# The first head's mask, in half of the key tiles, multiplied in by GpSimd after the exponential; both mask tables written by VectorE

## The chip, the core and the metric

The kernel runs on one core of a Trainium2 chip. The core has five engines with a queue each: TensorE (PE in the profile; its weight loads are PEld), VectorE (DVE), ScalarE (ACT), GpSimd (POOL) and SyncE (SP), which here only issues DMAs. They meet through semaphores. The metric is the device time of one execution in microseconds; smaller is better.

## The reference, cut to what matters

Four layers follow each other on `x` (4 batches, 512 queries, 256 features): a cross attention, an expert layer, a second cross attention with a mask over 1601 keys and 16 heads of 16 features, and a routed expert layer. The change touches the second cross attention alone:

```
energy = einsum('nqhd,nkhd->nhqk', qp, kp)                    # 4 batches, 16 heads, 512 x 1601
energy = where(mask == 0, -1e20, energy)
attention = softmax(energy / sqrt(256), axis=3)
out = einsum('nhql,nlhd->nqhd', attention, vp) @ fo_w.T + fo_b
```

The mask is one table of 512 x 1601 integers for each batch, the same for all its heads.

## The kernel before, in words

The second cross attention is the function `attention_c`. Its work is cut into 16 groups (`G` from 0 to 15; batch `b = G // 4`, and `g = G % 4` counts the four groups of four heads of a batch) and each group into 13 tiles of 128 keys (`i` from 0 to 12, the last with 65 keys). `T = 13 G + i` numbers the 208 tiles. For each tile and each of the four heads `h`, TensorE writes the scores, keys on the partitions and 512 queries along the free side, into one bank of PSUM (`score`, L2021); ScalarE takes the exponential with the scale in it into `prob` (L2189); and TensorE multiplies four heads' `prob` with the values, which carry a column of ones for the row sums (`values`, L2042). `prob` has two slots, one for each parity of `T`.

The exponential needs the row maximum. TensorE computes the scores of the *next* group a second time, queries on the partitions (`maximum`, L1995: 32 units `u` per group, two matmuls each), and VectorE adds the mask and takes the maximum of each unit (L2216, a main instruction and a read of its accumulator). Two units are under way at most: unit `m` waits on TensorE until VectorE is done with unit `m - 2`. At a group's end the maxima are split into three bf16 parts, turned and copied to the query rows, so that the score matmul subtracts them.

The mask comes into the scores in one of three ways, written down by `bank_plan` (L1613) for each tile and head in `MASKS`:

- `pe`: a matmul of an identity with the tile of `maskT` (0 or -1e20, bf16) opens the bank, and the score matmul adds to it (L2038, then L2039);
- `act`: ScalarE copies the tile of `maskT` into the bank ahead of the score matmul (L2185);
- `dve`: VectorE does so (L2306), in the last group only.

Over the 832 pairs of tile and head that is 498 `pe`, 310 `act` and 24 `dve`. Heads 0 and 1 are nearly always `pe`, heads 2 and 3 mostly `act`.

The order on TensorE within a tile is: scores of heads 0 and 1, a maximum unit, the values of the tile before, score of head 2, a maximum unit, score of head 3, a maximum unit. With three units per tile the 32 units are done after tile 10, and tiles 11 and 12 have none. Single jobs of the rest of the layer (turning outputs, projections, queries of the next batch, routing) lie between tiles of groups with `g` 0 and 1.

`maskT` is made from the integer mask, which is loaded two tiles at a time into one of two slots of `c_rawT`. GpSimd writes it (`bias_t`, L1908): all 13 tiles of batch 0 at the layer's start, and those of the next batch in group `g = 3` (tiles 2 to 10) and at the start of the following `g = 0`. GpSimd also scatters rows into `table` by indirect DMA for the routed layer (128 of them, L260), fills `table` with zeros in group 2 (16 DMAs, L1965, two each in tiles 2 to 9), copies values (L1874) and splits queries. Its loop over the tiles waits for the first score matmul of each tile, then runs `beside` (L1920).

## Time and profile before

| | before |
|---|---|
| median of 3 runs | 2099.51 us (2098.49 to 2099.77) |
| span of the profiled execution | 2122.9 us |
| the layer's tiles (first score matmul to last values) | 1100.9 to 1883.5 us of the span |
| busy in the span: PE / DVE / ACT / POOL | 1982.3 / 1269.1 / 893.8 / 528.3 us |
| VectorE maxima L2216 | 480 units, 467.7 us and 66.8 us of accumulator reads |
| ScalarE exponentials L2189 and mask copies L2185 | 832 and 310 |
| TensorE mask matmuls L2038 | 498 |
| GpSimd mask tiles L1913 | 52, 100.2 us |

The profile gives no other time for the profiled execution than its span; it is 23.4 us over the median of the runs. Matmuls are pipelined, so their durations overlap: what one costs TensorE is read as the distance from its start to the next start, not from its duration. The same holds, to a smaller degree, for ScalarE and VectorE.

### The profile page before, as it was taken

The numbers are of one execution on the slowest core, as the hardware profiler recorded it, in microseconds if no ns is written. First come the engines' busy times: TensorE is split into PE (matmuls) and PEld (weight loads), VectorE is DVE, ScalarE is ACT, GpSimd is POOL, SyncE is SP. The second block draws the span as 40 slices with busy tenths as digits, with TensorE's granted clock in tenths as the row PEclk, the third lists the DMA queues.
The fourth block names the chain that finished last, engine by engine and source line by source line (L and its number), as shares of the span: only waits on it lengthen the run. The fifth ranks groups of instructions, "written<-read, shape, count | busy, mean of one in ns | idle before, by whom it ended". The sixth has DMA issues, their size and how long they took to land. (4 is left out here: it accounts for less than half of the span.)

```text
span 2122.9 us, 27241 instructions
## 1 busy us (share of the span) xinstructions
PE 1982.3 (93%) x10186; PEld 1100.5 (52%) x10186; DVE 1269.1 (60%) x2541; ACT 893.8 (42%) x1791; POOL 528.3 (25%) x454
## 2 busy tenths in 40 slices
PE   7989999999999999899989999999999999965994
PEld 5666567745676567746643333433433343334773
DVE  5423765366633764367777777777776777741343
ACT  3412211221112211121118888778777977841221
POOL 4311000210001000000034223236324531426664
PEclk9999999999999999999999999999999999986997
DMA  8743000110001000110226383345335432215986
GB/s 286 213 200 111 1 1 11 45 43 1 1 21 62 1 1 11 34 28 16 44 79 129 85 259 81 80 120 123 90 70 146 104 57 43 73 62 164 251 182 157
DMA packets 101531, 184.97 MB, mean 87 GB/s; under 512 B 38151, under 2 KB 62549, under 8 KB 100120
## 3 DMA queue, kind: packets, MB, share of 16 engines
q1 hardware_dynamic: 83000, 153.24, 26.8%
q0 software_dynamic: 18400, 30.00, 6.3%
q8 instruction: 81, 1.33, 0.3%
q14 instruction: 50, 0.41, 0.1%
HBM read 127.38 MB, written 65.25 MB: 91 GB/s over the span
## 5 line engine op out<-in xcount | busy, mean ns | idle before, releaser
L2216 DVE CUSTOM_DVE_ANT_0 ps<-ps,maskN 128x801 f32<-128x801 f32 x480 | 467.7, 1014 | 129.5 <-PE ps L2009 126.3
L2189 ACT ACTIVATE d_prob<-ps 128x512 f32<-128x512 f32 (+1 forms) x832 | 473.4, 597 | 158.3 <-PE ps L2039 153.2
L856 PE MATMUL ps<-vx_or_keys,b_xT 128*128 128x512 f32 x512 | 240.3, 597 | 4.9 <-DVE val_or_prob L1209 4.9
L840 PE MATMUL ps<-oxB,og_or_pT 128*128 128x256 f32 x1024 | 241.1, 380 | 0.0
L2051 PE MATMUL ps<-d_prob,vaug 128*32 128x512 f32 (+1 forms) x1664 | 226.6, 610 | 0.3 <-ACT d_prob L2189 0.3
L840 PEld LDWEIGHTS ps<-oxB,og_or_pT 128*128 128x128 f32 x1024 | 190.5, 190 | 37.4 <-issue 11.2
L2038 PE MATMUL ps<-maskT,identb 128*128 128x512 bf16 (+1 forms) x498 | 192.2, 386 | 5.7 <-DVE d_oN L2248 1.7
L1095 ACT ACTIVATE prob_or_gate<-ps,b_mx 128x512 f32<-128x512 f32 (+3 forms) x128 | 66.1, 525 | 289.4 <-DVE b_mx L1200 289.4
L2185 ACT CAST ps<-maskT 128x512 f32<-128x512 bf16 (+1 forms) x310 | 185.6, 599 | 0.0
L260 POOL DMA_INDIRECT table<-xr,slot x128 | 128.6, 1005 | 177.5 <-PE ps L2039 140.8
L1209 DVE TENSOR_TENSOR val_or_prob<-ps,b_gm 128x512 f32<-128x512 f32 x128 | 88.4, 691 | 107.1 <-PE ps L856 107.0
L856 PEld LDWEIGHTS ps<-vx_or_keys,b_xT 128*128 128x128 f32 x512 | 93.5, 190 | 85.5 <-issue 77.5
L1213 DVE TENSOR_REDUCE val_or_prob<-val_or_prob 128x64 f32<-128x512 f32 x128 | 132.3, 1034 | 4.4
L2039 PE MATMUL ps<-raw,kS 99*128 99x512 bf16 (+1 forms) x312 | 115.7, 387 | 1.7 <-ACT ps L2185 1.7
L2038 PEld LDWEIGHTS ps<-maskT,identb 128*128 128x128 bf16 (+1 forms) x498 | 49.7, 100 | 123.0 <-issue 36.6
L1913 POOL TENSOR_SCALAR maskT<-c_rawT 128x512 bf16<-128x512 int32 (+1 forms) x52 | 100.2, 1926 | 49.0 <-PE ps L2039 42.2
L2039 PE MATMUL ps<-vx_or_keys 99*128 99x512 bf16 (+1 forms) x260 | 99.2, 385 | 1.9 <-ACT ps L2185 1.9
L2039 PE MATMUL ps<-qS,vx_or_keys 99*128 99x512 bf16 (+1 forms) x260 | 98.9, 384 | 1.9 <-ACT ps L2185 1.9
L670 PE MATMUL ps<-og_or_pT,raw 128*128 128x128 f32 (+1 forms) x832 | 97.6, 275 | 0.0
L640 PE MATMUL ps<-maskN,kS 128*128 128x512 f32 (+1 forms) x256 | 95.0, 519 | 1.7 <-PEq L98 1.7
L670 PEld LDWEIGHTS ps<-og_or_pT,raw 128*128 128x128 f32 (+1 forms) x832 | 95.4, 192 | 1.5 <-issue 1.5
L1332 DVE TENSOR_TENSOR og_or_pT<-b_oT,ps 128x512 f32<-128x512 f32 x128 | 81.9, 681 | 18.2 <-PE ps L814 18.2
(321 smaller groups left out, 2807.8 us busy)
## 6 DMA issues: line engine op xcount, KB each, us to landing
c_rawT<-in_maskT SPq DMA_DIRECT2D x24, 512.0 KB
vx_or_keys<-k_parts SPq DMA_DIRECT2D x60, 200.1 KB, 7.2
k_parts<-x_k SPq DMA_DIRECT2D x16, 600.4 KB
table<-xr POOLq DMA_DIRECT2D x16, 578.0 KB
e_buf<-table SPq DMA_DIRECT2D x32, 289.0 KB
raw<-in_mask SPq DMA_DIRECT2D x10, 800.5 KB, 4.2
vx_or_keys<-in_D_w SPq DMA_DIRECT2D x12, 640.0 KB, 5.5
e_w<-in_D_w SPq DMA_DIRECT2D x12, 640.0 KB
```

Of the source, the lines that this page charges most:

```text
L260: g.indirect_dma_start(out=k.table[:, :], out_offset=bass.IndirectOffsetOnAxis(ap=k.slot[:, j:j + 1], axis=0), in_=k.xr[:, t, :], in_offse ...
L670: mm = pe.matmul(ps[:, 6, m * P:(m + 1) * P], k.ctxNA[0:KW[i], i, m * P:(m + 1) * P], pT[0:KW[i], i, :], start=i == 0 and m == 0, stop=i = ...
L840: mm = pe.matmul(ps[:, 6 + t // 2, (t % 2) * D:(t % 2 + 1) * D], og[:, e, t * P:(t + 1) * P], oxB[:, p, e, :], start=first and t % 2 == 0, ...
L856: mm = pe.matmul(ps[:, bank, :], xTB[:, c, t * P:(t + 1) * P], vxB[:, c, h, :], start=c == 0, stop=c == NC - 1)
L1213: v.tensor_reduce(val[:, t, h // 2 % 2, h % 2, :], tmp[:, u % 2, :].rearrange("p (e d) -> p d e", e=EB), AX_X, ALU.add).then_inc(val_sum, 1)
L1913: g.tensor_scalar(maskT[0:KW[i], i, :], rawT[0:KW[i], u % 2, i % 2, :], 0.0, MASKED, ALU.is_equal, ALU.mult).then_inc(biasT, 1)
L2038: pe.matmul(ps[0:w, BANKS[u], :], k.identb[0:w, 0:w], maskT[0:w, i, :], start=True, stop=False)
L2039: pe.matmul(ps[0:w, BANKS[u], :], kS[G % NS][0:KROWS + 3, h, i * P:i * P + w], qS[G % NS][0:KROWS + 3, h, :], start=False, stop=True, skip ...
L2051: mm = pe.matmul(ps[VW * h:VW * (h + 1), ACC, :], vaug[0:w, G % 2, i, h, :], prob[0:w, T % 2, h, :], start=i == 0, stop=i == NKT - 1)
L2185: nc.scalar.copy(ps[0:w, BANKS[later], :], maskT[0:w, i, :]).then_inc(mask_a, 1)
L2189: nc.scalar.activation(prob[0:w, T % 2, h, :], ps[0:w, BANKS[GH * T + h], :], ACT.Exp, scale=SCALE_C).then_inc(exped, 1)
L2216: v.tensor_tensor_reduce(banks, banks, maskN[:, t, MO[half]:MO[half] + w], 1.0, -3.0e38, ALU.add, ALU.max, mp[:, t, h, half:half + 1]).the ...
```

## The change

A fourth way of masking, `cap`, is used for head 0 in 108 of the 208 tiles (`capped_by_gpsimd`). There TensorE writes the score of head 0 without a mask matmul, ScalarE takes the exponential of the unmasked score, and GpSimd then goes over the 128 x 512 tile of `prob` twice, in place: it bounds it by 2 and multiplies it by the tile of a second table `capsT` (1 for a seen key, 2^-100 for a hidden one). `values` waits for that (`capped`). In tiles with `i` divisible by 4 that are capped, head 2's mask goes from ScalarE's copy to TensorE's matmul. Both tables are written by VectorE, two instructions per tile, between its maxima: in group 0 two tiles ahead and then one behind each of the first 11 units; in groups with `g = 3` of batches 0 to 2 one behind every third unit from 6 to 30; and one behind units 2, 5, 8 and 11 of the following group. GpSimd's scatters are moved to tiles that are not capped. The tile into which `x` is loaded is now the one that holds the last `x` (`k.xl`). Over the pairs the plan now has 410 `pe`, 290 `act`, 24 `dve` and 108 `cap`.

```diff
@@ -1610,6 +1611,20 @@
+def capped_by_gpsimd(T):
+    G, i = divmod(T, NKT)
+    b, g = divmod(G, NG)
+    if g == 0:
+        return i != 12 and (b < 2 or i % 2 == 0 or i > 5)
+    if g == 1:
+        return 5 <= i <= 10
+    if g == 2:
+        return i >= 2 and (b == 0 or b + 1 < NB and i in (4, 6, 8, 10))
+    return b == 0 or b + 1 < NB and i in (2, 4, 6, 8, 10)
@@ -1650,11 +1665,15 @@
-                by = "pe"
-                if bank in whole:
+                by, cap = "pe", capped_by_gpsimd(NKT * G + i)
+                if h == 0 and cap:
+                    by = "cap"
...
-                    elif i >= 1 and G < NGB - 1 and h >= 2:
+                    elif i >= 1 and G < NGB - 1 and h >= (3 if cap and i % 4 == 0 else 2):
                         by = "act"
@@ -1905,13 +1931,18 @@
+            def cap(T):
+                by, count = MASKS[GH * T]
+                if by == "cap":
+                    w, i = KW[T % NKT], T % NKT
+                    p = prob[0:w, T % 2, 0, :]
+                    g.wait_ge(exped, GH * T + 1)
+                    g.tensor_scalar(p, p, 2.0, None, ALU.min).then_inc(bounded, 1)
+                    g.wait_ge(bounded, count)
+                    g.wait_ge(capT, NKT * (T // NKT // NG) + i + 1)
+                    g.tensor_tensor(p, p, capsT[0:w, i, :], ALU.mult).then_inc(capped, 1)
@@ -1933,17 +1964,19 @@
+                    if a == 2 and i >= 2 and b + 1 < NB:
+                        many = [1, 2, 0, 2, 0, 2, 0, 2, 0, 2, 1]
+                        scatters(b, sum(many[:i - 2]), many[i - 2])
+                    if a == 3 and b + 1 < NB:
+                        many = [1, 2, 0, 2, 0, 2, 0, 2, 0, 2, 0, 2, 1]
...
@@ -1974,21 +2005,17 @@
             for T in range(NKT * NGB):
                 g.wait_ge(s_mm, GH * T + 1)
                 beside(T // NKT // NG, T // NKT % NG, T % NKT)
+                cap(T)
@@ -2037,12 +2066,14 @@
                 pe.matmul(ps[0:w, BANKS[u], :], kS[G % NS][0:KROWS + 3, h, i * P:i * P + w], qS[G % NS][0:KROWS + 3, h, :],
-                          start=False, stop=True, skip_group_check=by != "pe").then_inc(s_mm, 1)
+                          start=by == "cap", stop=True, skip_group_check=by in ("act", "dve")).then_inc(s_mm, 1)
             def values(T):
                 pe.wait_ge(exped, GH * (T + 1))
+                if MASKS[GH * T][0] == "cap":
+                    pe.wait_ge(capped, MASKS[GH * T][1])
@@ -2269,13 +2300,34 @@
+            def bias_t(b, i):
+                u, w = NP * b + i // 2, KW[i]
+                v.wait_ge(ld_maskT[u % 2], 16 * (u // 2 + 1))
+                if b >= 1:
+                    v.wait_ge(s_mm, GH * (NKT * (NG * b - 1) + i + 1))
+                raw = rawT[0:w, u % 2, i % 2, :]
+                v.tensor_scalar(maskT[0:w, i, :], raw, 0.0, MASKED, ALU.is_equal, ALU.mult).then_inc(biasT, 1)
+                if b >= 1:
+                    v.wait_ge(capped, caps_until(NKT * (NG * b - 1) + i))
+                v.tensor_scalar(capsT[0:w, i, :], raw, 0.0, HIDDEN, ALU.not_equal, ALU.max).then_inc(capT, 1)
...
+                    if G == 0 and u < NKT - 2:
+                        bias_t(0, u + 2)
+                    if g == 3 and b + 1 < NB and 6 <= u <= 30 and u % 3 == 0:
+                        bias_t(b + 1, u // 3 - 2)
+                    if g == 0 and b >= 1 and u <= 11 and u % 3 == 2:
+                        bias_t(b, 9 + u // 3)
```

On TensorE, in tile 1 of group 0, this stood in a row before (L2038 mask, L2039 score, L2009 maximum, L2051 values):

```order
L2038 MATMUL ps<-maskT,identb 128x512
L2039 MATMUL ps<-raw,kS 128x512
L2038 MATMUL ps<-maskT,identb 128x512
L2039 MATMUL ps<-raw,kS 128x512
L2009 MATMUL ps<-vx_or_keys 128x512
L2009 MATMUL ps<-vx_or_keys 128x288
L2051 MATMUL ps<-d_prob,vaug 32x512 x4
```

and this stands there now (L2067 mask, L2068 score, L2082 values):

```order
L2068 MATMUL ps<-raw,kS 128x512
L2067 MATMUL ps<-maskT,identb 128x512
L2068 MATMUL ps<-raw,kS 128x512
L2040 MATMUL ps<-vx_or_keys 128x512
L2040 MATMUL ps<-vx_or_keys 128x288
L2082 MATMUL ps<-d_prob,vaug 32x512 x4
```

One mask matmul of the two ahead of the maximum is gone. On VectorE, at the start of group 0, the maxima (two rows each, `ISA`) followed each other directly before:

```order
L2237 COPY raw<-ps 3x1024 x2
L2216 ISA ps,d_mp<-ps,maskN 128x801
L2216 ISA d_mp 128x1
L2216 ISA ps,d_mp<-ps,maskN 128x800
L2216 ISA d_mp 128x1
```

and now have two pairs of table writes ahead of them and one pair behind each:

```order
L2268 COPY raw<-ps 3x1024 x2
L2311 TENSOR_SCALAR maskT<-c_rawT 128x512
L2314 TENSOR_SCALAR capsT<-c_rawT 128x512
L2311 TENSOR_SCALAR maskT<-c_rawT 128x512
L2314 TENSOR_SCALAR capsT<-c_rawT 128x512
L2247 ISA ps,d_mp<-ps,maskN 128x801
L2247 ISA d_mp 128x1
L2311 TENSOR_SCALAR maskT<-c_rawT 128x512
L2314 TENSOR_SCALAR capsT<-c_rawT 128x512
L2247 ISA ps,d_mp<-ps,maskN 128x800
L2247 ISA d_mp 128x1
```

The pairs go on behind each of the first 11 units, and stand behind every third one in the groups with `g = 3`. On GpSimd, in group 2, the 16 fills of `table` stood around one copy of values before:

```order
L1965 DMA table<-xr 128x1156 x6
L1874 COPY vaug<-c_vg 128x52x16
L1965 DMA table<-xr 128x1156 x10
```

and each two of them now stand ahead of the two passes over a capped tile:

```order
L1996 DMA table<-xr 128x1156
L1996 DMA table<-xr 128x1156
L1942 TENSOR_SCALAR d_prob<-d_prob 128x512
L1945 TENSOR_TENSOR d_prob<-d_prob,capsT 128x512
```

The two passes come behind what `beside` issues in the same tile.

## Rows read from the trace of the kernel before

**Rows 1.** Timeline of TensorE, group 7: start and duration (us), engine, line, operation.
```profile
1456.45 1.06 PE L2051 MATMUL ps<-d_prob,vaug 128*32 128x512 f32 x8
...
1458.59 0.38 PE L2038 MATMUL ps<-maskT,identb 128*128 128x512 bf16 x1
1458.81 0.38 PE L2039 MATMUL ps<-vx_or_keys 99*128 99x512 bf16 x1
...
1459.46 0.51 PE L2009 MATMUL ps<-vx_or_keys,qS 96*128 96x512 bf16 x2
1459.90 1.07 PE L2051 MATMUL ps<-d_prob,vaug 128*32 128x512 f32 x8
1460.89 0.39 PE L2039 MATMUL ps<-vx_or_keys 99*128 99x512 bf16 x1
```

**Rows 2.** Timeline of ScalarE and VectorE in the same tile.
```profile
1459.14 1.03 DVE L2216 CUSTOM_DVE_ANT_0 ps<-ps,maskN 128x800 f32<-128x800 f32 x1
1459.22 0.60 ACT L2189 ACTIVATE d_prob<-ps 128x512 f32<-128x512 f32 x1 [0.18 <-PE ps L2039]
...
1459.72 0.59 ACT L2185 CAST ps<-maskT 128x512 f32<-128x512 bf16 x1
...
1460.09 1.03 DVE L2216 CUSTOM_DVE_ANT_0 ps<-ps,maskN 128x801 f32<-128x801 f32 x1
1460.23 0.60 ACT L2189 ACTIVATE d_prob<-ps 128x512 f32<-128x512 f32 x1
...
1461.32 1.16 ACT L2189 ACTIVATE d_prob<-ps 128x512 f32<-128x512 f32 x2
...
1461.67 1.00 DVE L2216 CUSTOM_DVE_ANT_0 ps<-ps,maskN 128x800 f32<-128x800 f32 x1 [0.49 <-PE ps L2009]
```

**Rows 3.** Who waited for whom, TensorE, 1100 to 1883 us: total, times, longest.
```profile
PE ps L2009 <- DVE d_mp L2216: 12.1, 17, 2.4
PE ps L2039 <- ACT ps L2185: 5.6, 12, 0.5
```

**Rows 4.** Timeline of ScalarE: copies of the accumulator, behind groups 2 and 3.
```profile
1253.12 0.59 ACT L2181 COPY d_acc<-ps 128x512 f32<-128x512 f32 x1 [0.61 <-PE ps L2051]
...
1298.26 0.59 ACT L2181 COPY d_acc<-ps 128x512 f32<-128x512 f32 x1 [0.61 <-PE ps L2051]
```

**Rows 5.** Timeline of VectorE: a narrow table write; one of 1601 between maxima.
```profile
1378.15 0.23 DVE L326 TENSOR_SCALAR cr_selb<-cr_rest 128x128 bf16<-128x128 f32 x1
...
1412.91 1.00 DVE L2216 CUSTOM_DVE_ANT_0 ps<-ps,maskN 128x800 f32<-128x800 f32 x1 [0.49 <-PE ps L2009]
...
1414.07 1.00 DVE L2270 TENSOR_SCALAR maskN<-raw 128x1601 bf16<-128x1601 int32 x1
1414.98 0.99 DVE L2216 CUSTOM_DVE_ANT_0 ps<-ps,maskN 128x801 f32<-128x801 f32 x1
```

**Rows 6.** Timeline of the layer's start, TensorE, VectorE, GpSimd.
```profile
1100.91 0.61 PE L2038 MATMUL ps<-maskT,identb 128*128 128x512 bf16 x1 [1.61 <-POOL maskT L1913]
...
1103.51 1.00 DVE L2216 CUSTOM_DVE_ANT_0 ps<-ps,maskN 128x801 f32<-128x801 f32 x1 [2.86 <-PE ps L2009]
...
1117.58 0.51 PE L2009 MATMUL ps<-vx_or_keys 96*128 96x512 bf16 x2
...
1127.54 2.76 POOL L1968 MEMSET vx_or_keys<- 3x3204 f32 x1
1130.39 2.36 POOL L1888 TENSOR_TENSOR d_xb<-c_x,boC 128x1024 f32<-128x1024 f32 x1
```

**Rows 7.** Groups by line and form, GpSimd: count | busy us, mean ns | idle before.
```profile
L1913 POOL TENSOR_SCALAR maskT<-c_rawT 128x512 bf16<-128x512 int32 x48 | 92.5, 1926 | 46.8 <-PE ps L2039 40.2 <-DMA c_rawT<-in_maskT 2.0 <-DMA c_vg<-v_all 1.7
...
L1901 POOL TENSOR_TENSOR c_rest<-c_xn,c_q 128x512 f32<-128x512 f32 x6 | 6.9, 1158 | 0.5
...
L1899 POOL CAST c_q<-c_xn 128x512 bf16<-128x512 f32 x6 | 3.7, 614 | 88.4 <-ACT c_xn L2169 83.0 <-PE ps L2039 5.4
```

**Rows 8.** Timeline of GpSimd, group 2: the two fills of one tile.
```profile
1216.83 1.05 POOL L1965 DMA_DIRECT2D table<-xr  x2 [3.20 <-PE ps L2039]
```

**Rows 9.** Timeline, VectorE beside GpSimd, at the layer's start and in group 6.
```profile
1095.21 1.53 DVE L1431 CAST d_m<-d_m 128x16 bf16<-128x16 f32 x1
1095.22 1.49 POOL L1974 MEMSET vaug<- 128x1664 f32 x1
...
1144.59 0.18 DVE L1431 CAST d_m<-d_m 128x16 bf16<-128x16 f32 x1
...
1445.77 0.99 DVE L2270 TENSOR_SCALAR maskN<-c_rawN 128x1601 bf16<-128x1601 int32 x1
1446.00 1.61 POOL L260 DMA_INDIRECT table<-xr,slot  x1 [0.85 <-PE ps L2039]
1447.91 0.97 POOL L260 DMA_INDIRECT table<-xr,slot  x1 [0.30 <-issue]
```

## What the change should do to the time

> **What bounds the kernel now.** I read the timeline of one tile of a group without side jobs first, since the busy shares say nothing on where the slack is. On TensorE a mask matmul and a score matmul start 0.22 us apart, the values take 0.99 us from start to next start, and the values of one tile start 3.45 us after those of the last [rows 1]. Six matmuls of 0.22, three maximum units of about 0.35, the 0.99 and 0.09 between a maximum and the values make 3.44 us: the tile is full. ScalarE in the same tile has 0.18 us idle ahead of the first exponential, and its instructions start 0.5 us (a copy behind an exponential or the reverse) to 0.55 us apart: four exponentials and two copies need 3.1 us [rows 2]. VectorE starts maxima 0.95 us apart when they wait for nothing, 2.85 us for three, and idles 0.6 us in a tile [rows 2]. So TensorE sets the pace, ScalarE is 0.34 us behind, VectorE 0.6 us. The list of waits agrees: TensorE lost only 12.1 us to the maxima and 5.6 us to ScalarE's copies in 782 us [rows 3]. A group of such tiles lasts 45.1 us [rows 4]. GpSimd, off the path, had 528 of 2122.9 us of work.
>
> **What the change removes.** 88 mask matmuls leave TensorE (498 to 410) and 20 copies leave ScalarE (310 to 290). A matmul is worth 0.22 us. The ceiling is thus 88 x 0.22 = 19 us. Less of it counts:
> - 6 sit in tiles 11, which have no maxima and where ScalarE's 3.1 us bound; they give nothing. 82 are left.
> - 25 sit in stretches where VectorE will set the pace (next part): 4 in tiles 0 to 3 of group 0, 7 in tiles 2 to 10 of group 3, 3 each in groups 7 and 11, and 8 in tiles 0 to 3 of groups 4, 8 and 12. They give nothing. 57 are left.
> - About 10 of these are in tiles beside routing or query jobs, where TensorE already waits for VectorE or for data. 47 x 0.22 = 10.3 us.
> - The exchange of a copy for a matmul (tiles divisible by 4) gives TensorE nothing, since a copy leaves ScalarE and the matmul count stays as it was. Only tile 12 of groups 2 and 3, bound by ScalarE, gain 0.5 us each: 1.0 us.
>
> Sum: -11 us. With 0.22 us less on TensorE a tile needs 3.22 us, still over ScalarE's 3.1.
>
> **What it adds on VectorE.** 104 table writes of 128x512. The trace has the operation at 1601 elements and at 128: 1.00 and 0.23 us [rows 5], so 0.52 ns an element, and 0.43 us for 512. What matters is the time that VectorE loses. Between two maxima a write of 1601 made their starts 2.07 us apart instead of 0.95 [rows 5]: 0.22 us to get going behind the accumulator read and 0.91 us from start to start. For a pair of 512 that is 0.22 + 2 x 0.34 = 0.90 us. Bounds: below, no loss at all where VectorE idles 0.6 us; above, 2 x 0.43 + 0.22 = 1.1 us.
> - Group 0, 11 units with a pair each: VectorE needs 0.95 + 0.90 = 1.85 us a unit. Its first maximum started at 1103.5; I leave that, as the two pairs ahead fit before it. The eleventh (u = 10) is then done at 1103.5 + 10 x 1.85 + 1.06 = 1123.1. Unit 12 may not start on TensorE before, and started at 1117.58 [rows 6]. Loss 5.5 us. It isn't won back, for TensorE is full behind it.
> - Groups 3, 7 and 11, a pair in each of nine tiles: 2.85 + 0.90 = 3.75 us against 3.44, so 9 x 0.31 = 2.8 us; the first takes up some slack: 2.4 us each, 7.2 us.
> - Groups 4, 8 and 12, four pairs: tile 1 loses 0.31, tile 2 about 0.6 because `outputs` is there as well, tile 3 about 0.1: 1 us each, 3 us.
>
> Sum: +15.7 us.
>
> **What it adds on GpSimd.** Two passes over 128x512. The multiply is as L1901: 1.16 us. The bound has no row; a copy of the same size takes 0.61, a two-operation pass 1.93 us [rows 7]. I take 1.1 us, nearer to the copy, for it has one operation where L1913 has two and reads no integers. With two waits of about 0.1 us a tile costs 2.45 us (2.0 to 3.3). TensorE needs it before the values, which start about 3.5 us after the first exponential ends (next tile's scores, a unit, in rows 1 and 2: 1459.82 and 1463.3). So it's hidden in most tiles, and scatters are never in a capped tile. Not in group 2: fills take 1.05 us of each of tiles 2 to 9 [rows 8], and 1.05 + 2.45 + waits make 3.6 to 3.7 us against 3.44 of before, 8 x 0.25 less the slack that it starts with: +1.5 us.
>
> **What neither queue shows alone.** At 1095.21 a VectorE cast of 16 elements took 1.53 us instead of 0.18, and ended with the GpSimd memset that ran beside it; at 1446.00 an indirect DMA of GpSimd took 1.61 instead of 0.97 us while VectorE wrote a mask row [rows 9]. The maxima, whose operands lie in PSUM but for the mask, are 0.97 to 1.04 us long throughout. So a table write on VectorE and an instruction on GpSimd seem to take turns. Before, they hardly met. Now GpSimd is busy 2.3 of some 3.7 us in a capped tile, and a write that comes at random waits 0.6 x 0.56 = 0.35 us. Group 0: 22 writes beside caps at some 0.2 us, and at its start the memset of 2.76 and the sum of 2.36 us [rows 6] that GpSimd runs just when VectorE begins its tables: together 2 to 6 us. Group 3: 18 x 0.25 = 4.5 us. Groups 7 and 11: 8 writes each beside caps, 4 us. The rest: 2 us. That makes 0 to 17 us; I take 9, since waits that overlap a wait for TensorE cost nothing.
>
> The Trainium skill has this as a rule (SBUF — State Buffer, section "SBUF: two separate sides"): the port pair that VectorE and GpSimd share is locked for a whole instruction, and the other "fully blocks". By the rule the sum is that with this part, and without it the result would be the second rival's; the two rows agree with the rule, though no row shows it for a table write against an elementwise GpSimd pass.
>
> **The sum.** On the profiled execution: 2122.9 - 11 + 15.7 + 1.5 + 9 = 2138 us of span. The median of the runs is 23.4 us below the span of before, and I carry the difference of 15 us over: 2099.5 + 15 = 2114.5 us.
>
> **Rivals.**
> - No taking turns. If table writes and GpSimd's passes don't hinder each other, the sum is -11 + 15.7 + 1.5 = +6: 2105.5 us. For it: GpSimd's L1913 had 1.93 us each time, beside any number of maxima. Against it: rows 9.
> - Faster. VectorE's 0.6 us of idle time and the two units in flight hide most of the pairs in groups 3 to 12, so that only group 0's 5.5 us is left and 70 or so of the matmuls count (-15): 2090 us. For it: the single row of 1601 in a tile is not twice as dear as its 0.5 us over the slack. Against it: the pair comes in every tile, and 3.75 us is more than 3.44. It decides where a pair costs under 0.6 us.
> - GpSimd bounds. If the bound costs 1.9 us, a capped tile takes 3.3 us of GpSimd, and every tile of batch 0 goes at 3.4 to 3.5 us, those with fills at 4.4: 8 x 0.75 = 6 us more, and the 25 matmuls gained in batch 0 are lost: 6. 2126 us. For it: L1913. Against it: it has twice the operations.
>
> **How the numbers follow.** Forecast 0.45, no taking turns 0.23, faster 0.15, GpSimd 0.17. A measurement tells a difference from none at about 0.2%, 4.2 us here: below 2095.3 is faster, above 2103.7 slower. The forecast spreads over 2104 to 2122, the second case over 2099 to 2110, with a third of it under 2103.7; of the third case 0.05 lies above 2095.3, and the forecast has 0.04 below 2103.7. So faster 0.11, same 0.18, slower 0.71. The range is 2097 to 2130.
>
> **What would show it.** Right: table writes of about 0.43 us, some over 1 us beside a GpSimd pass; TensorE's waits for L2216 (now L2247) up from 12 us to over 30 us; group 0 five to ten us longer; groups 7 and 11 at 47.5 to 50 us instead of 45.1; groups 13 and 5 about 1 us shorter; a GpSimd tile of 2.4 us. Wrong: groups 3, 7, 11 not longer than before; values waiting for the multiply in most capped tiles.

## The result, and the profile after

The kernel after the change ran at 2162.41 us, median of 4 runs (2161.32 to 2163.45), beside 2099.64 us for the kernel before (2098.49 to 2103.68): a ratio of 1.0294, 95% interval 1.028 to 1.0308. The forecast was 2114.5 us with a range to 2130. The sign was right; the size was four times too small.

Both kernels ran again later: after at 2181.40 against 2122.77 us, ratio 1.0265 (1.0248 to 1.0283). The same kernel thus took 1% longer in a later set of runs. The chip of the first set is not on record, so the cause stays open. The 23.4 us between the median and the profile's span that I took for a property of the profile is most likely such a difference: in every later profile the span was about 2 us *below* the run's own time. The table by groups below is made on the later profiles, where the two agree; the rows of after are from its first profile, unless said otherwise.

The page of after has these rows, in its usual form (line, operation, count, then busy us and mean ns, then idle before and what ended it). They answer to [rows 3], [rows 5] and [rows 7].

```profile
PE 1973.5 (91%) x9997; PEld 1087.2 (50%) x10098; DVE 1333.3 (62%) x2645; ACT 881.7 (41%) x1771; POOL 720.6 (33%) x618
L2082 PE MATMUL ps<-d_prob,vaug 128*32 128x512 f32 (+1 forms) x1664 | 230.0, 619 | 27.3 <-POOL d_prob L1945 25.8
L1942 POOL TENSOR_SCALAR d_prob<-d_prob 128x512 f32<-128x512 f32 (+1 forms) x108 | 164.9, 1527 | 133.9 <-ACT d_prob L2220 133.5
L1945 POOL TENSOR_TENSOR d_prob<-d_prob,capsT 128x512 f32<-128x512 f32 (+1 forms) x108 | 125.7, 1164 | 9.0
```

The same for the waits of TensorE between 1101 and 1936 us (total, times, longest):

```profile
PE ps L2036 <- DVE d_mp L2247: 34.1, 47, 3.9
PE ps L2082 <- POOL d_prob L1945: 25.8, 8, 8.3
PE ps L2068 <- ACT ps L2216: 5.9, 12, 0.6
```

The maxima (L2247) held TensorE 34.1 us where it was 12.1 before [rows 3]; that was forecast. The second row was not: the values waited for GpSimd's multiply eight times only, for 0.3 to 8.3 us. One of the eight, on GpSimd and then TensorE, around tiles 5 and 6 of group 0:

```profile
1142.89 0.88 POOL L1900 COPY vaug<-c_vg 128x832 f32<-128x832 f32 x1 [8.67 <-DMA c_vg<-v_all]
1143.73 1.48 POOL L1942 TENSOR_SCALAR d_prob<-d_prob 128x512 f32<-128x512 f32 x1
1145.30 1.15 POOL L1945 TENSOR_TENSOR d_prob<-d_prob,capsT 128x512 f32<-128x512 f32 x1
```
```profile
1146.60 1.94 PE L2082 MATMUL ps<-d_prob,vaug 128*32 128x512 f32 x8 [7.40 <-POOL d_prob L1945]
1148.47 0.61 PE L2068 MATMUL ps<-raw,kS 99*128 99x512 bf16 x1
```
```profile
1130.00:1140.00 10.00, 8.51 (x45) 2.54 (x44) 9.58 (x21) 7.63 (x15) 2.78 (x2) 1.00 1.04 136
1140.00:1150.00 10.00, 3.40 (x13) 0.84 (x14) 0.75 (x3) 1.04 (x2) 6.08 (x5) 0.56 0.40 88
1150.00:1160.00 10.00, 9.84 (x54) 3.15 (x53) 8.45 (x17) 8.28 (x16) 6.29 (x5) 0.93 0.01 2
```

Read it from the top. GpSimd copies the next group's values in tile 5 of each group (`values_of`, in `beside`), and that copy stood 8.67 us for the DMA that brings them. The two passes over tile 5 are queued behind it. TensorE stood 7.40 us for the second of them, and everything that feeds on TensorE stood with it. The windows (length, busy us of PE, PEld, DVE, ACT, POOL, then granted clock, DMA share, GB/s) show TensorE busy for 3.40 of 10 us, and its granted clock at 0.56 in that stretch, so about at the lower level of 1.2 GHz for much of it: the first matmuls after the stall took 1.94 and 0.61 us instead of 1.06 and 0.38 [rows 1].

The table compares the groups, as the time between ScalarE's copies of the accumulator [rows 4], in the later profiles; group 0 counts from its first matmul, a mask matmul before and with the tables alone, a score matmul in the others. Groups 14 and 15 never differ by more than 0.02.

| group | before | after | values early | tables alone | mask left out |
|---|---|---|---|---|---|
| 0 | 51.88 | 72.06 | 63.17 | 57.00 | 51.76 |
| 1 | 49.89 | 48.91 | 48.90 | 49.89 | 48.89 |
| 2 | 53.00 | 61.01 | 56.35 | 47.61 | 47.51 |
| 3 / 7 / 11 | 45.14 / 45.15 / 45.15 | 50.20 / 49.32 / 49.33 | 50.19 / 49.32 / 49.31 | 45.29 / 45.34 / 45.34 | 44.44 / 45.12 / 45.12 |
| 4 / 8 / 12 | 51.27 / 51.27 / 50.72 | 55.41 / 53.11 / 50.69 | 51.96 / 51.45 / 50.68 | 51.70 / 51.70 / 51.13 | 50.07 / 50.72 / 49.94 |
| 5 / 9 / 13 | 55.41 / 55.41 / 51.32 | 55.26 / 56.93 / 55.28 | 55.25 / 56.92 / 53.65 | 55.41 / 55.40 / 51.33 | 54.56 / 54.54 / 50.68 |
| 6 / 10 | 49.56 / 49.92 | 52.76 / 52.84 | 47.05 / 47.08 | 47.02 / 47.00 | 52.28 / 50.49 |

After less before is 58 us in these groups, and 58.6 us in the medians of the later runs: the difference lies in the layer that was changed, as far as one profile of each can tell. How far that is shows in the first profile of after, where the layer was 8.3 us shorter: groups 2 and 4 were 2.3 and 2.2 us shorter, group 5 took 56.94 and group 8 51.45 us. Group 9 took 55.24 us. The 1.7 us in groups 5 and 9 goes with TensorE's clock. In both profiles both groups have a wait of 1.69 us for the maxima. Behind it the granted clock over 10 us was 0.83 to 0.85, so partly at the lower level of 1.2 GHz, where the group was long, and 1.00, so at 2.4 GHz, where it was short. A difference of 1.6 or 1.7 us in one group of one profile is therefore no effect of an edit by itself.

### The profile page after: what moved, and what is told of

It reads as the page before. It is cut to its first block and busy times, and to the rows that moved or that the text cites. A ratio compares the mean times of both kernels' runs of the same rounds, so it can differ in the third digit from the quotient of the medians.

```text
span 2161.6 us, 27513 instructions
## 1 busy us (share of the span) xinstructions
PE 1973.5 (91%) x9997; PEld 1087.2 (50%) x10098; DVE 1333.3 (62%) x2645; ACT 881.7 (41%) x1771; POOL 720.6 (33%) x618
## 5 line engine op out<-in xcount | busy, mean ns | idle before, releaser
L2247 DVE CUSTOM_DVE_ANT_0 ps<-ps,maskN 128x801 f32<-128x801 f32 x480 | 467.1, 1012 | 128.1 <-PE ps L2036 127.0
L2082 PE MATMUL ps<-d_prob,vaug 128*32 128x512 f32 (+1 forms) x1664 | 230.0, 619 | 27.3 <-POOL d_prob L1945 25.8
L1942 POOL TENSOR_SCALAR d_prob<-d_prob 128x512 f32<-128x512 f32 (+1 forms) x108 | 164.9, 1527 | 133.9 <-ACT d_prob L2220 133.5
L2216 ACT CAST ps<-maskT 128x512 f32<-128x512 bf16 (+1 forms) x290 | 173.9, 600 | 0.0
L2067 PE MATMUL ps<-maskT,identb 128*128 128x512 bf16 (+1 forms) x337 | 130.4, 387 | 3.1 <-DVE d_oN L2279 3.0
L1945 POOL TENSOR_TENSOR d_prob<-d_prob,capsT 128x512 f32<-128x512 f32 (+1 forms) x108 | 125.7, 1164 | 9.0
L2068 PE MATMUL ps<-raw,kS 99*128 99x512 bf16 (+1 forms) x312 | 116.9, 392 | 7.2 <-DVE maskT L2311 1.9
L2068 PE MATMUL ps<-vx_or_keys 99*128 99x512 bf16 (+1 forms) x260 | 99.5, 387 | 4.5 <-ACT ps L2216 1.9
L2068 PE MATMUL ps<-qS,vx_or_keys 99*128 99x512 bf16 (+1 forms) x260 | 98.3, 384 | 4.6 <-ACT ps L2216 2.1
L2067 PEld LDWEIGHTS ps<-maskT,identb 128*128 128x128 bf16 (+1 forms) x410 | 40.5, 99 | 121.4 <-issue 40.1
L2036 PE MATMUL ps<-vx_or_keys 96*128 96x512 bf16 x320 | 84.8, 347 | 17.9 <-DVE d_mp L2247 17.2
```

What stands on the lines that cost most here:

```text
L1942: g.tensor_scalar(p, p, 2.0, None, ALU.min).then_inc(bounded, 1)
L1945: g.tensor_tensor(p, p, capsT[0:w, i, :], ALU.mult).then_inc(capped, 1)
L2067: pe.matmul(ps[0:w, BANKS[u], :], k.identb[0:w, 0:w], maskT[0:w, i, :], start=True, stop=False)
L2068: pe.matmul(ps[0:w, BANKS[u], :], kS[G % NS][0:KROWS + 3, h, i * P:i * P + w], qS[G % NS][0:KROWS + 3, h, :], start=by == "cap", stop=True ...
L2082: mm = pe.matmul(ps[VW * h:VW * (h + 1), ACC, :], vaug[0:w, G % 2, i, h, :], prob[0:w, T % 2, h, :], start=i == 0, stop=i == NKT - 1)
L2216: nc.scalar.copy(ps[0:w, BANKS[later], :], maskT[0:w, i, :]).then_inc(mask_a, 1)
```

## The experiments

**The kernel before, once more**

> The kernel before once more, for its profile. The changed kernel's profile has a span of 2161.6 us and its runs take 2162.4, while the first profile of before had 2122.9 us against runs of 2099.6. If that profile holds a disturbance of about 23 us in the expert layer (TensorE idle from 1925 to 1951 us), this one has a span of about 2098 us, the last copy of the accumulator at 1883 to 1884 us and no such stall. If the stall belongs to the kernel, the span is 2122 again.

It ran at 2130.22 us with a span of 2128.4 us, where I had expected 2098; before had a median of 2123.38 us in the runs of this set. What follows the layer's last copy took 241 us here and 239 us in the first profile, so there was no passing stall of 23 us behind the layer. Nor has the kernel before a fixed distance between span and median. It is its own reference on each chip, and only ratios are carried from one chip to another.

**Values loaded early**

```diff
             load_x(0)
+            load_v(1)
...
                 b, g = divmod(G, NG)
+                if 1 <= G < NGB - 1:
+                    load_v(G + 1)
                 if G >= 1:
...
-                if G + 1 < NGB:
-                    load_v(G + 1)
```

> The changed kernel with one edit: SyncE issues the load of the next group's values one group earlier, ahead of the loads of keys, queries and mask tiles. Theory 1 (queue): in tile 5 of each group GpSimd's copy of these values waits for that DMA, and the two passes over the capped tile stand behind it in the queue, so TensorE's values wait (25.8 us in 8 waits, and TensorE at half clock for some microseconds behind them). Then these waits go, and the time falls by 28 to 36 us, to 2126 to 2134. Theory 2 (VectorE): VectorE's table writes and their turns with GpSimd set the pace in groups 0 to 3 anyway, so what is won at tile 5 is lost again: 2150 to 2162.

2153.38 us, ratio 1.0139 (1.0114 to 1.0164). Against after's later 1.0265 this is some 27 us, just under the 28 to 36 of the first theory. The copy on GpSimd now waits for its turn alone, and tile 5 is like any other:

```profile
1134.64 0.88 POOL L1901 COPY vaug<-c_vg 128x832 f32<-128x832 f32 x1 [2.01 <-PE ps L2069]
1135.49 1.49 POOL L1943 TENSOR_SCALAR d_prob<-d_prob 128x512 f32<-128x512 f32 x1
1137.06 1.16 POOL L1946 TENSOR_TENSOR d_prob<-d_prob,capsT 128x512 f32<-128x512 f32 x1
```

By groups the saving is 8.9 in group 0, 4.7 in 2, 3.5 in 4, 5.7 and 5.8 in 6 and 10, and 1.7 in 8; each of them has a wait for the multiply in after. The 1.6 in group 13 is not the edit's: two other versions with early values have 55.2 us there. That makes 30 us, and 22 against the first profile of after, which has no such wait in group 8 and shorter ones in 2 and 4. Groups 3, 7 and 11 didn't move by more than 0.02. The queue is one cause, and not the only one.

**Tables alone**

```diff
 def capped_by_gpsimd(T):
+    return False
```

> The changed kernel without any capped tile: all masks by matmul and copy as before, but VectorE writes both tables. It measures VectorE's part. My sum had 15.7 us for it without turns (5.5 in group 0, 2.4 in each of groups 3, 7 and 11, 1 in each of groups 4, 8, 12): 2115 us. Since GpSimd is nearly idle there, turns should be rare except at the start (the memset of 2.8 us and the sum of 2.4 us), 2 to 4 us more. Rival: VectorE's slack hides the pairs outside group 0: 2106 to 2109.

2127.01 us, ratio 1.0017 (1.0004 to 1.003), so 3.6 us where my sum had 15.7 and the rival 6.5 to 9.5. VectorE writes both tables, no pass is made. Group 0 is 5.1 us longer (5.5 forecast), but groups 3, 7 and 11 only 0.15 to 0.2 (2.4 forecast), and 4, 8 and 12 only 0.4 (1 forecast). The 5.1 us is a net of two things. Before had a wait of VectorE for x in this group, which is absent here and in the kernel before with its loads moved (below). From the same score matmul that version takes 48.93 us and this one 56.60, so the tables cost 7.7 us. Some 4.4 of them are lost at the start: the second maximum starts 8.5 us behind the group's first matmul, where it was 4.1, because two table writes stand beside GpSimd's memset and sum:

```profile
1104.39 2.04 DVE L2301 TENSOR_SCALAR maskT<-c_rawT 128x512 bf16<-128x512 int32 x1
1106.36 2.56 DVE L2304 TENSOR_SCALAR capsT<-c_rawT 128x512 bf16<-128x512 int32 x1
```

**Mask of head 0 left out**

```diff
+                if h == 0 and cap:
+                    by = "cap"
...
-                          start=False, stop=True, skip_group_check=by != "pe").then_inc(s_mm, 1)
+                          start=by == "cap", stop=True, skip_group_check=by in ("act", "dve")).then_inc(s_mm, 1)
```

> The kernel before with the new plan of masks and no passes of GpSimd: in the 108 tiles head 0's mask is left out of the computation altogether, and GpSimd writes maskT as before. It measures what 88 fewer mask matmuls and 20 fewer copies are worth by themselves. My sum said 11 us where VectorE's pairs take some away; here those stretches count too, so 14 to 17 us: 2083 to 2086. Rival: ScalarE is right behind TensorE (3.1 us of 3.44 in a tile), so that less than half shows: 2092 to 2097.

It is the kernel before with the new plan alone: the mask of head 0 is left out in the 108 tiles, there are no passes and no `capsT`. 2120.91 us, ratio 0.9982 (0.997 to 0.9995). This is what the change removes, with nothing added: 2.5 us in the runs, where I had expected 14 to 17; the rival, that less than half shows, was right. The profile, in the groups that no stall disturbs, has 6.7 us: 1.0 in group 1, 0.7 in 3, 1.2, 0.55 and 0.8 in 4, 8 and 12, 0.85, 0.87 and 0.64 in 5, 9 and 13, 0.1 in 0, and nothing in 7 and 11. So even free of charge the masking on GpSimd would have gained about 0.1 to 0.3%.

**After, once more**

> The changed kernel once more, beside runs of before on the same chip as the kernels of this call. In the profiles the attention layer ends 52.4 us later than before, and the rest of the program differs by the chip (the expert layer took 225.7 us behind the changed kernel and 241 us behind the kernel before on another chip). If the change costs only in the attention layer, the ratio here is (before + 50 to 54 us) / before, about 1.024 to 1.026. If the expert layer pays as well (it should not, its code and queues are the same), it is 1.028 or more.

2181.40 us, ratio 1.0265 (1.0248 to 1.0283). TensorE's waits are those of the first profile: 34.6 us for the maxima, 28.4 us for the multiply in 8 pieces. The ratio lies between my two cases. What follows the layer took 241 us here as in the repeated profile of before, so the expert layer pays nothing; the layer's own difference was 58 us, not 50 to 54.

**No tables for batches 1 to 3**

```diff
-                    if g == 3 and b + 1 < NB and 6 <= u <= 30 and u % 3 == 0:
-                        bias_t(b + 1, u // 3 - 2)
-                    if g == 0 and b >= 1 and u <= 11 and u % 3 == 2:
-                        bias_t(b, 9 + u // 3)
```

> The kernel of e1 (values loaded early) with the table writes and mask loads of batches 1 to 3 left out: these batches use batch 0's tables. The caps stay, those of groups 3, 7 and 11 too. In e1 these groups are 4.0 to 4.9 us longer than with tables and no caps (50.2, 49.3, 49.3 against 45.3), and without caps the tables cost only 0.2 us each. Theory 1 (turns): VectorE's table writes wait for GpSimd's passes, so without the writes groups 3, 7 and 11 fall to 44.4 to 45.1 us, as with the mask left out: 12 to 14 us less than e1 in all. Theory 2 (GpSimd's latency): the passes come too late for the values by themselves; the groups stay at 48 us or more.

On top of the early values, the later batches keep batch 0's masks, and the loads of their mask tiles are gone too. 2131.66 us, ratio 1.0033 (1.002 to 1.0045). Groups 3, 7 and 11 took 44.45, 45.12 and 45.14 us, with all passes in place, which is what the mask left out had. Tables without passes cost them 0.2 us, passes without tables nothing, both together 4.2 to 5.1 us. The price is in their meeting: in the version with early values the 18 table writes of each of these groups took 5.3, 5.0 and 5.0 us longer than 0.415 us each. In all this version is 22 us below the one with early values, not the 12 to 14 expected. Group 2 alone fell from 56.35 to 50.56 us, for the loads of its mask tiles are gone, and with them VectorE's wait of 4.94 us for a mask row.

**One pass instead of two**

```diff
-                    g.tensor_scalar(p, p, 2.0, None, ALU.min).then_inc(bounded, 1)
-                    g.wait_ge(bounded, count)
                     g.wait_ge(capT, NKT * (T // NKT // NG) + i + 1)
```

> The kernel of e1 with the bounding pass left out in all 108 tiles, so a capped tile costs GpSimd 1.16 us instead of 2.7. Theory 1 (GpSimd is full in group 2, where two fills and two passes take 3.87 us a tile against the 3.44 of before): group 2 falls from 56.4 us to 48 to 50. Theory 2 (the waits for the mask rows' DMA make group 2 long, as in the kernel before): it stays over 54. In groups 3, 7 and 11 GpSimd is busy half as long, so by the turns about half of their 4 to 5 us goes: 46.5 to 48 us each. In all 12 to 16 us less than e1.

The bound is left out, the multiply stays. 2141.92 us, ratio 1.0081 (1.0066 to 1.0096), 12 us below the version with early values, as expected, but not where I expected it. Group 2 did not fall to 48 to 50 us: it took 57.08, with a wait of 7.04 us on VectorE for a mask row. The first theory failed there. Groups 3, 7 and 11: 45.27, 45.47 and 45.46 us. Half of GpSimd's time would by my random meeting have left half of the cost; nothing was left. The timelines say why. After, group 3, VectorE and then GpSimd:

```profile
1305.65 0.13 DVE L2247 DVE_READ_ACCUMULATOR2_ANT d_mp<- 128x1 f32 x1
1305.65 0.94 DVE L2311 TENSOR_SCALAR maskT<-c_rawT 128x512 bf16<-128x512 int32 x1
1306.51 0.41 DVE L2314 TENSOR_SCALAR capsT<-c_rawT 128x512 bf16<-128x512 int32 x1
...
1309.65 1.05 DVE L2311 TENSOR_SCALAR maskT<-c_rawT 128x512 bf16<-128x512 int32 x1
1310.62 0.41 DVE L2314 TENSOR_SCALAR capsT<-c_rawT 128x512 bf16<-128x512 int32 x1
```
```profile
1303.58 1.48 POOL L1942 TENSOR_SCALAR d_prob<-d_prob 128x512 f32<-128x512 f32 x1 [1.28 <-ACT d_prob L2220]
1305.15 1.15 POOL L1945 TENSOR_TENSOR d_prob<-d_prob,capsT 128x512 f32<-128x512 f32 x1
1307.69 1.48 POOL L1942 TENSOR_SCALAR d_prob<-d_prob 128x512 f32<-128x512 f32 x1 [1.39 <-ACT d_prob L2220]
1309.26 1.16 POOL L1945 TENSOR_TENSOR d_prob<-d_prob,capsT 128x512 f32<-128x512 f32 x1
```

The first write of each pair starts inside the multiply (1305.15 to 1306.30) and ends 0.3 us behind it, at 1306.59; the second one is undisturbed. This comes again in the next tile, 4.0 us later, and so on: eight of the nine pairs in group 3 have a write of over 0.7 us, and the median of the nine first writes is 0.94 us. In groups 7 and 11, where every second tile has passes, it is every second pair. With one pass, the same two engines:

```profile
1294.34 0.42 DVE L2310 TENSOR_SCALAR maskT<-c_rawT 128x512 bf16<-128x512 int32 x1
1294.68 0.42 DVE L2313 TENSOR_SCALAR capsT<-c_rawT 128x512 bf16<-128x512 int32 x1
...
1297.82 0.43 DVE L2310 TENSOR_SCALAR maskT<-c_rawT 128x512 bf16<-128x512 int32 x1
```
```profile
1292.89 1.16 POOL L1944 TENSOR_TENSOR d_prob<-d_prob,capsT 128x512 f32<-128x512 f32 x1 [2.32 <-ACT d_prob L2219]
1296.38 1.16 POOL L1944 TENSOR_TENSOR d_prob<-d_prob,capsT 128x512 f32<-128x512 f32 x1 [2.32 <-ACT d_prob L2219]
```

The pass ends at 1294.05, 0.3 us before the write. It was luck of the phase, repeated nine times, and not a share of time. The meeting turned up elsewhere instead. In group 4, VectorE and then GpSimd with one pass:

```profile
1317.17 1.30 DVE L2310 TENSOR_SCALAR maskT<-c_rawT 128x512 bf16<-128x512 int32 x1
```
```profile
1317.04 1.16 POOL L1944 TENSOR_TENSOR d_prob<-d_prob,capsT 128x512 f32<-128x512 f32 x1 [2.39 <-ACT d_prob L2219]
```

All four pairs of that group have a write of 1.08 to 1.38 us, where the version with early values had 0.56 to 0.83, and groups 4, 8 and 12 took 54.09, 52.49 and 51.73 us, so 2.1, 1.0 and 1.0 us longer.

**Mask rows loaded first, in the kernel before**

```diff
                 if g == 2 and b + 1 < NB:
-                    load_maskT(b + 1, 0)
-                    load_maskT(b + 1, 1)
                     load_maskN(b + 1, 2)
                     load_maskN(b + 1, 3)
+                    load_maskT(b + 1, 0)
+                    load_maskT(b + 1, 1)
```

> The kernel before with one edit in SyncE's order in groups with g = 2: the two loads of mask rows stand ahead of the two loads of mask tiles, not behind them. In group 2 of before VectorE waited 1.9 and 3.5 us for the third mask row in two profiles, TensorE stood still for 3.9 us and then ran at half clock for about 5 us (group 2 lasted 50.2 and 53.0 us, 47.5 in kernels where the row came in time). If the row comes in time, group 2 takes 47.5 us, 3 to 5 us less, and the whole 0.15 to 0.25% less. Rival: the DMA engines are full with the fills of the table at that time (share over 1.0), so the order changes nothing, or the stall moves to the mask tiles.

2120.88 us, ratio 0.999 (0.9978 to 1.0001): not told from no change. Group 2 fell to 47.00 us, but 6 and 10 were at 50.74 and 51.37. The edit aims at a wait of 1.85 and 3.49 us in the two profiles of before, which the version with early values shows too, on VectorE in group 2:

```profile
1248.77 1.00 DVE L2302 TENSOR_SCALAR maskN<-raw 128x1601 bf16<-128x1601 int32 x1 [4.94 <-DMA raw<-in_mask]
```

**Early values, and no passes in groups 3, 7 and 11**

```diff
-    return b == 0 or b + 1 < NB and i in (2, 4, 6, 8, 10)
+    return False
```

> The kernel with the values loaded early, and head 0 of groups 3, 7 and 11 masked by TensorE or ScalarE as before; the passes of the other groups and all table writes stay. Nothing of the computation is left out. My theory (the table writes and GpSimd's passes cost groups 3, 7 and 11 their length only by meeting, as the runs without tables and with one pass each suggest): 50.19, 49.32 and 49.31 us fall to about 45.3 each, so the time falls by 4.9 + 4.0 + 4.0 = 12.9 us against the version with early values, from a ratio of 1.0139 to 1.0078. Rival (the conflict only moves, since the scatters of GpSimd in these groups meet the same table writes): each group keeps 1 to 2 us over 45.3, and the ratio is 1.0095 or more. A third (the tables alone are dear where nothing else changes, by my first estimate 2.4 us a group): 47.5 each, ratio 1.011.

2140.31 us, ratio 1.0073 (1.0051 to 1.0095). The groups took 45.28, 45.34 and 45.34 us: the conflict is gone, it didn't move, and the ratio is the 1.0078 of the first theory within its interval. The interval also touches the 1.0095 of the rival; the groups exclude it.

**Both edits of the loads, in the kernel before**

```diff
+            load_v(1)
...
+                if 1 <= G < NGB - 1:
+                    load_v(G + 1)
...
-                if G + 1 < NGB:
-                    load_v(G + 1)
...
-                    load_maskT(b + 1, 0)
-                    load_maskT(b + 1, 1)
                     load_maskN(b + 1, 2)
                     load_maskN(b + 1, 3)
+                    load_maskT(b + 1, 0)
+                    load_maskT(b + 1, 1)
```

> The kernel before with two edits of the loads: the next group's values are loaded ahead of keys and queries, and the mask rows ahead of the mask tiles in groups with g = 2. It is the control for the fitted version. My theory: TensorE never waited for the values' copy before, so the first edit gives nothing: ratio 0.998 to 1.000, as with the mask rows alone (0.999), group 2 at 47.0 us, GpSimd's copies of the values without a wait. Rival (the early load displaces the keys' load, for which the maxima wait): some group's start is 1 us or more longer, ratio over 1.001.

2115.52 us against 2127.23 us, ratio 0.9945 (0.9928 to 0.9962). It beats both kernels, and I was wrong to give the first edit nothing. Group 0 is 2.6 us shorter (48.93 against 51.50, both from the first score matmul that the profiles show), group 2 is at 46.91, 6 and 10 at 47.05 and 47.02. For group 0 the timelines give the reason; x is loaded behind those values, and VectorE's statistics waited for it. Before (first profile), then with the loads moved:

```profile
1139.81 1.41 DVE L131 BATCH_NORM_STATS2 norm_nc_stats<-c_x 128x6 f32<-128x256 f32 x4 [1.75 <-DMA c_x<-x_mid]
```
```profile
1139.65 1.41 DVE L131 BATCH_NORM_STATS2 norm_nc_stats<-c_x 128x6 f32<-128x256 f32 x4
```

With that wait goes one of 2.26 us on TensorE, at 1144.49 in the repeated profile of before. In group 6 of before all engines stood for 2 to 3 us at about 1445; the profile puts it down to "remote" on ScalarE (2.90 us) and GpSimd (2.04 us), which says nothing of the cause. Groups 6 and 10 are 2.5 and 2.9 us longer there. None of the six profiles with early values has this, but neither has the one with the tables alone. So what the stall is, and whether the edit or chance keeps it away, stays open; 5.4 us of the 14 us that these two profiles differ by in the layer rest on it. In the runs the gain is 11.7 us, or 0.55%.

**A fitted version**

```diff
     if g == 0:
-        return i != 12 and (b < 2 or i % 2 == 0 or i > 5)
+        return b >= 1 and 6 <= i <= 11
     if g == 1:
-        return 5 <= i <= 10
-    if g == 2:
-        return i >= 2 and (b == 0 or b + 1 < NB and i in (4, 6, 8, 10))
-    return b == 0 or b + 1 < NB and i in (2, 4, 6, 8, 10)
+        return b >= 1 and 5 <= i <= 10
+    return False
```

> A version drawn from the experiments, with nothing of the computation left out: values loaded early, mask rows loaded ahead of mask tiles, batch 0 as before (GpSimd writes maskT, no head is masked by GpSimd), and in batches 1 to 3 head 0 is masked by GpSimd in tiles 6 to 11 of the first group and 5 to 10 of the second alone, so that no pass stands beside a table write or a fill. My theory: group 0 at 51.8 us, group 2 at 47.0, groups 3, 7 and 11 at 45.3, groups 4, 8 and 12 0.4 longer for the tables and 0.4 shorter for the mask matmuls, groups 5 and 9 0.5 shorter; where no stall falls into groups 6 and 10 they are at 47.0. Layer 0 to 8 us shorter, ratio 0.996 to 1.0. Rival (each pass costs TensorE about what its matmul gave back, by waits that I have not named): ratio 1.000 to 1.003 and no gain over the version with the loads alone.

Both edits of the loads, batch 0 as before, and passes only where no table write and no fill of `table` stands. 2117.84 us, ratio 0.9961 (0.9944 to 0.9977): faster than before, but by its loads. Beside them alone (2115.52 us on the same chip) it has nothing. Its groups 4, 8, 5 and 9 are 0.1 to 0.2 us shorter, 12 is 0.3, and group 13 is 55.28 against 51.33 us. Here is VectorE, and GpSimd beside it, in the fitted version, and below VectorE with the loads alone:

```profile
1770.56 0.96 DVE L332 TENSOR_TENSOR xr<-cr_e,cr_dn 128x128 f32<-128x128 f32 x1
...
1781.44 0.81 DVE L369 TENSOR_SCALAR slot<-cr_nearest 128x32 int32<-128x32 f32 x1
```
```profile
1770.22 1.15 POOL L1950 TENSOR_TENSOR d_prob<-d_prob,capsT 128x512 f32<-128x512 f32 x1
...
1781.06 1.16 POOL L1950 TENSOR_TENSOR d_prob<-d_prob,capsT 128x512 f32<-128x512 f32 x1
```
```profile
1771.46 0.29 DVE L331 TENSOR_TENSOR xr<-cr_e,cr_dn 128x128 f32<-128x128 f32 x1
...
1779.97 0.18 DVE L368 TENSOR_SCALAR slot<-cr_nearest 128x32 int32<-128x32 f32 x1
```

Two small steps of the routing, 0.29 and 0.18 us long alone, ended with GpSimd's multiply, 0.96 and 0.81 us long. TensorE waited 2.04 and 1.69 us for the maxima behind them, where it was 1.27 and 0.78 us with the loads alone. That is 1.7 of the 3.95 us. Behind the longer waits the clock fell too: granted 0.83 in the fitted version between 1772 and 1792 us, so in part at 1.2 GHz, and 1.00 in the other. I take the other 2.3 us to be that. It agrees with the version with early values, where the clock stayed at 1.00 behind the second of these waits and the group took 53.65 us.

## Why the prediction was right in sign and wrong in size

- **The bound.** TensorE sets the pace of a plain tile, with ScalarE close behind: right for the tile. In groups 7 and 11 the removed matmuls gave nothing all the same.
- **Removed, -11 us.** Mis-sized. The layer's undisturbed groups gave 6.7 us, the runs 2.5 us. A removed matmul was not worth 0.22 us. That ScalarE, 0.34 us behind, is the next to be late is my reading; no run shows it.
- **Tables, +15.7 us.** Group 0's +5.5 was +5.1, and that is luck: 7.7 us were lost and the 2.6 us of a wait for x were won. Of the 7.7, 4.4 are from writes beside the memset and the sum, which I had put under the turns; the pairs alone cost 3.3. The 7.2 and 3 of the others were 0.5 and 1.3 us. The failed term is the price of a pair in my sum, 0.90 us. I had read 0.22 us "to get going behind the accumulator read" from the write of a mask row [rows 5]. But `bias_n` waits there for a semaphore of the maxima (`mx_v`), and `bias_t` has no such wait, which fits the gap. In after the first write starts *with* the accumulator read, and an undisturbed pair moves the next maximum from 1117.54 to 1118.21, so 0.67 us. Three units and such a pair need 2.85 + 0.67 = 3.52 us, 0.08 over the tile's 3.44 where I had 0.31. The bound of "no loss at all" was the right end of the range, and the "faster" rival had this part right:

```profile
1117.54 0.13 DVE L2247 DVE_READ_ACCUMULATOR2_ANT d_mp<- 128x1 f32 x1
1117.54 0.42 DVE L2311 TENSOR_SCALAR maskT<-c_rawT 128x512 bf16<-128x512 int32 x1
1117.88 0.41 DVE L2314 TENSOR_SCALAR capsT<-c_rawT 128x512 bf16<-128x512 int32 x1
1118.21 0.99 DVE L2247 CUSTOM_DVE_ANT_0 ps<-ps,maskN 128x801 f32<-128x801 f32 x1
```

- **GpSimd's passes.** The multiply took 1.16 us as said, the bound 1.49 us in place of 1.1, between the 0.61 and 1.93 us of the rows that I went by. A capped tile costs 2.7 us, not 2.45. In group 2, with two fills in 1.15 us, GpSimd was full (3.9 to 4.7 us from one bounding pass to the next without the tables of later batches). There the group took 50.56 us against 47.61 us with the tables alone. That is 3.0 us where I had 1.5. The rest of group 2's length is a wait for a DMA: of the values in after, of a mask row with early values and with one pass.
- **"So it's hidden in most tiles."** This step failed, and it is the largest part of the miss: 27 us by the runs, 22 or 30 us by the groups, of 58. I checked what *scatters* stand ahead of a pass and not what the other work there waits for. The trace of before held the answer, in GpSimd's copy of the values:

```profile
1138.79 0.88 POOL L1874 COPY vaug<-c_vg 128x832 f32<-128x832 f32 x1 [6.04 <-DMA c_vg<-v_all]
```

  Nothing that TensorE needed soon stood behind it then. The change put a pass there that TensorE needs within 3.5 us. A wait without cost on an idle engine became a wait on the path, and the clock fell after it.
- **Taking turns, +9 us.** The mechanism is shown, by the runs with each side alone (0.2, 0, and 4.2 to 5.1 us together) and by writes that end just behind GpSimd's instruction. The rule that the forecast names from the Trainium skill (SBUF — State Buffer, section "SBUF: two separate sides"), one side holds the shared ports for a whole instruction and the other waits, agrees with these rows. The size was three times too small. Groups 3, 7 and 11 cost 4.9, 4.0 and 4.0 us against 4.5, 2 and 2 forecast. Group 0 lost 4.4 us at its start by the memset and the sum that I had named; the two writes are as long in after (below) as with the tables alone. It lost 6.2 us more with passes and early values, and the 20 writes behind the start are 5.7 us longer there. With the 4 us of group 13, where routing steps meet passes and the clock falls, that is some 27 us against 9. Not foreseen were group 13 and the lock of phase.

```profile
1106.35 2.04 DVE L2311 TENSOR_SCALAR maskT<-c_rawT 128x512 bf16<-128x512 int32 x1
1108.32 2.56 DVE L2314 TENSOR_SCALAR capsT<-c_rawT 128x512 bf16<-128x512 int32 x1
```
```profile
1105.18 2.93 POOL L1999 MEMSET vx_or_keys<- 3x3204 f32 x1
1108.19 2.40 POOL L1914 TENSOR_TENSOR d_xb<-xl,boC 128x1024 f32<-128x1024 f32 x1
```

- **What would show it.** Waits for the maxima over 30 us: yes. Groups 7 and 11 between 47.5 and 50: yes, 49.3. Group 0 five to ten us longer: no, 20. Group 5 one shorter: 0.15 in one profile, 1.5 longer in the other; group 13: 4 longer. Values waiting in most capped tiles: no, in eight tiles; I had looked for many short waits and there were a few long ones.
- **The rivals.** "No turns", which the sentence on the rule calls the second rival, fell with the runs above. "GpSimd bounds" was right only in group 2. "Faster" had the tables of the later groups right, and would have needed free passes and twice the gain from the matmuls: it had 15 us for them, where the mask left out gave 6.7.

## What to carry to other kernels

Before work that another engine needs is put on an idle engine's queue, read every wait of that queue, however harmless: each can become a wait of the path, and here the cure was to issue a load earlier. VectorE and GpSimd both working on SBUF didn't meet at random here but in step with the tile: in a group the meeting came in nearly every tile with passes, or in none. A shorter pass removed it from groups 3, 7 and 11 and made it dearer in 4, 8 and 12, so read all groups before calling it gone. And time first what the removal alone is worth: here the mask left out gained 0.18%, so there was next to nothing to pay for its replacement.

## What the runs showed of the hardware

- One kernel took 2099.6 us in one set of runs and 2122.8, 2123.4 and 2127.2 us in three later ones, each on another chip; the chip of the first is not on record.
- An elementwise GpSimd pass with one input (bound, 128x512 f32 in place) took 1.49 us, longer than the multiply of two inputs with 1.16 us.
- VectorE's table write of 128x512 took 0.41 us alone. In the rows above, a VectorE instruction that meets a GpSimd one ends 0.03 to 0.3 us behind it: a write of 0.41 us took 0.94, a step of 0.18 us took 0.81, and a GpSimd pass is held up as well: 1.68 and 1.66 us instead of 1.49 at 1110.56 and 1113.49 in group 0 of after. The maxima, which read PSUM, stayed at 0.97 to 1.03 us in both profiles of after but for six of 1.04.
- TensorE's granted clock was 0.56 over the 10 us that held a stall of 7.4 us, and 0.93 over the next 10. Behind the same wait of 1.69 us it was 1.00 over 10 us in some groups and 0.83 to 0.85 in others, and the group was then 1.6 to 1.7 us longer.
